# Token index stored behind each row, a new order of the first steps, and x of eight tiles transposed by VectorE through DRAM

## The reference

```
tid = clip(token_ids, 0, 24999);  expert = min(tid // 6250, 3)
h   = layernorm(x)
g   = silu(h @ ctx[e].T);  u = h @ ctx[e].T;  y = (g * u) @ ctx[e]      # e: the token's expert
x   = x + tanh(g_xattn) * y
h   = layernorm(x)                                                      # second half
out = x + tanh(g_ffn) * ((silu(h @ gate.T * gate_s) * (h @ up.T * up_s)) @ down.T * down_s)
```

## Time and profile before

| | |
|---|---|
| time, median of 3 runs (range) | 388.78 us (388.47 to 388.99) |
| profiled execution, its own time | 389.44 us |
| its span, first to last instruction | 387.7 us |
| TensorE busy | 373.1 us, 96% |
| VectorE busy | 243.5 us, 63% |
| ScalarE busy | 147.1 us, 38% |
| GpSimd busy | 81.8 us, 21% |
| DMA | 40.91 MB, mean 106 GB/s |

### The profile page before, as it was taken

The page is one execution under the profiler, slowest core; times in us unless marked ns, Lnnn a source line. Parts: engine busy times, 40 slices in busy tenths (PEclk is TensorE's granted clock), DMA queues, the critical chain, the costliest instruction groups (busy, mean ns, idle before and its releaser), DMA issues.

```text
span 387.7 us, 5617 instructions
## 1 busy us (share of the span) xinstructions
PE 373.1 (96%) x1757; PEld 303.1 (78%) x1757; DVE 243.5 (63%) x455; ACT 147.1 (38%) x265; POOL 81.8 (21%) x108
## 2 busy tenths in 40 slices
PE   3999999999999999999999999999999999999992
PEld 2477788888888878888888888888888888888891
DVE  6888856667877678778847255747246757222253
ACT  4355556565545346422332223332222332222220
POOL 7523443434352120010002101002101001200011
PEclk9999999999999999999999999999999999999997
DMA  6775666663221126333201322200232300100011
GB/s 221 258 253 191 248 216 253 210 216 102 89 68 68 56 86 216 97 119 81 83 0 54 135 80 83 71 11 31 88 124 62 101 27 27 81 0 0 0 41 73
DMA packets 21905, 40.91 MB, mean 106 GB/s; under 512 B 2672, under 2 KB 8816, under 8 KB 21888
## 3 DMA queue, kind: packets, MB, share of 16 engines
q1 hardware_dynamic: 17536, 26.50, 21.3%
q0 software_dynamic: 4352, 14.19, 9.8%
HBM read 28.36 MB, written 12.32 MB: 105 GB/s over the span
## 4 chain that ended last, share of the span: by engine, by line
PE 93%; DVE 3%; POOL 1%; issue 1%; ACT 0%; DVEq 0%; POOLq 0%
PE bank L1149 40%; PE bank L1045 26%; PE bank L1156 20%; PE bank L1031 2%; PE bank L1060 2%; PE bank L1073 1%; POOL minus_j L362 1%; PE bank L1021 0%; DVE rows L934 0%; PE bank L1012 0%; DVE tmp L927 0%; DVE xn L927 0%; DVE is_low L647 0%; PE bank L1083 0%; DVE sh L882 0%
## 5 line engine op out<-in xcount | busy, mean ns | idle before, releaser
L1149 PE MATMUL bank<-work,wgu 128*128 (+1 forms) x736 | 167.3, 380 | 0.0
L1149 PEld LDWEIGHTS bank<-work,wgu 128*128 128x128 f32 x736 | 133.9, 188 | 27.1 <-issue 0.5
L1045 PE MATMUL bank<-work,parts 128*128 (+1 forms) x432 | 110.7, 402 | 0.8 <-ACT parts L463 0.2
L1045 PEld LDWEIGHTS bank<-work,parts 128*128 128x128 f32 x432 | 78.5, 188 | 20.0 <-issue 2.9
L1156 PE MATMUL bank<-work,hp 128*128 128x512 f32 x352 | 87.2, 390 | 0.2 <-DVE hp L886 0.2
L1156 PEld LDWEIGHTS bank<-work,hp 128*128 128x128 f32 x352 | 65.7, 188 | 14.4 <-DVE hp L886 0.6
L867 DVE SCALAR_TENSOR_TENSOR sh<-bank,gs,sh 128x512 f32<-128x512 f32 x42 | 31.5, 749 | 55.6 <-PE bank L1149 55.6
L567 ACT ACTIVATE hp<-sh 128x512 fp32r<-128x512 f32 x42 | 26.6, 634 | 78.7 <-DVE sh L867 78.7
L562 ACT ACTIVATE sh<-bank,gs 128x512 f32<-128x512 f32 x42 | 28.9, 689 | 71.6 <-PE bank L1149 68.8
L391 POOL TENSOR_TENSOR rstd<-ve,half 128x1 f32<-128x1 f32 x31 | 18.1, 583 | 124.3 <-DVE ve L708 124.3
L446 POOL DMA_INDIRECT out<-rows,oidx x16 | 16.2, 1011 | 128.0 <-DVE rows L934 105.8
(11 more groups left out here) (132 smaller groups left out, 267.4 us busy)
## 6 DMA issues: line engine op xcount, KB each, us to landing
wraw<-guT SPq DMA_DIRECT2D x8, 704.0 KB
ctx_in<-ctxT SPq DMA_DIRECT2D x4, 1024.0 KB, 6.1
rows<-x_rows SPq DMA_DIRECT2D x8, 512.0 KB, 4.4
turned_rows<-xn SPq DMA_DIRECT2D x12, 256.0 KB, 2.7
rows<-turned_rows SPq DMA_DIRECT2D x12, 256.0 KB, 2.7
checked<-dwT SPq DMA_DIRECT2D x11, 256.0 KB
rows<-dwT SPq DMA_DIRECT2D x11, 256.0 KB, 2.9
rows<-x,gidx POOLq DMA_INDIRECT x19
```

Of the source, the lines that this page charges most:

```text
L1045: mm = pe.matmul(out_ps[:, :], part(s)[:, c * P:(c + 1) * P], ctx_w(e, c, w), start=n == 0, stop=n == last)
L1149: mm = pe.matmul(out_ps[:, tiles.start * P:tiles.stop * P], wgu[:, row + h, w, c * P:(c + 1) * P], moving, start=n == 0, stop=n == last)
```

## The change

- **Index behind each row.** Rows in SBUF and in the scratch tensor grow from 512 to 528 words (`WIDE`). GpSimd copies the token's index into word 512 of its slot (`token_in`); it travels with the row, and the last scatter reads it there. `oidx`, its VectorE operations, its 16 matmuls and the wait for it go away.
- **First steps.** Seven of the 16 low parts of the expert matrices move to GpSimd (`ON_POOL`); the nine left on VectorE are placed one by one, all but the last five ahead of x of tile 0's low part. x of tile 0 is normalised, transposed, rounded and subtracted in two halves, in two PSUM banks. `keep_busy` runs 11 and 2 matmuls instead of 15 and 3.
- **x of tiles 11 to 18** (`ON_PE` = 11) is no longer transposed by TensorE: norm(k+2) writes it in a permuted order, SP writes it to DRAM and reads it back (`turn_rows(0)` to `turn_rows(7)`), VectorE transposes 32x32 blocks (`turn`), ScalarE and VectorE split it (`turned_hi`, `turned_lo`). From step 10 on normalisation and statistics run one tile further ahead.
- **What is moved.** `first_stats(0)` and `(1)` both stand ahead of step 9, the other two behind steps 11 and 13. On SP the two halves of the load of block 0 are apart: one ahead of check row 8, the other behind `turn_rows(0)`; all eight `turn_rows` stand ahead of the down rows.

```diff
+WIDE = D + 16
+ON_PE = 11
+AHEAD = STEPS - ON_PE
+ON_POOL = [(1, 2), (1, 3), (2, 0), (2, 1), (2, 2), (3, 0), (3, 1)]
-    scratch = nc.dram_tensor("x1_rows", [2 * TOKENS + STEPS * P, D], F32).ap()
+    scratch = nc.dram_tensor("x1_rows", [2 * TOKENS + STEPS * P, WIDE], F32).ap()
-        rows = sb("rows", [P, ROWS, D], F32)
+        rows = sb("rows", [P, ROWS, WIDE], F32)
...
 (SP)
+            load_half(0, 0)
             check_row(8)
-            load_rows(0)
-            for c in range(9, IC):
-                check_row(c)
+            turn_rows(0)
+            load_half(0, 1)
+            check_row(9)
+            turn_rows(1)
+            check_row(10)
+            for n in range(2, AHEAD):
+                turn_rows(n)
...
 (GpSimd)
+            def ctx_lo(n_from, n_to):
+                for n in range(n_from, n_to):
+                    e, c = ON_POOL[n]
+                    pool.wait_ge(S["ctx_hi"], KC * e + c + 1)
+                    pool.tensor_tensor(ctx_w(e, c, 1), ctx_in[:, e, c, :], ctx_w(e, c, 0).bitcast(F32),
+                                       ALU.subtract).then_inc(S["pool_ctx_lo"], 1)
+            token_in(0, 2)
+            token_in(2, 4)
             inverse_std(1)
+            pool.wait_ge(S["xn_ready"], 2)
+            ctx_lo(0, 2)
+            inverse_std(2)
             gather(4)
-            inverse_std(2)
+            pool.wait_ge(S["xn_ready"], 3)
+            ctx_lo(2, 5)
+            inverse_std(3)
...
             store(0)
+            ctx_lo(5, 7)
             for k in range(2, STEPS + 1):
-                if k + 2 < STEPS:
+                if k < ON_PE:
                     inverse_std(k + 2)
...
                     gather(k + 4)
+                    token_in(k + 4)
+                if ON_PE - 1 <= k < STEPS - 3:
+                    inverse_std(k + 3)
...
 (VectorE)
+            def last_on_pe(k):
+                h_lo(k - 1)
+                norm(k + 1, ring_slot(k + 1))
+                landed(k + 2)
+                stats(k + 2, ring_slot(k + 2))
+                hidden(k)
+                x_lo(k + 1)
+                norm(k + 2, ring_slot(k + 2))
+                update(k - 1)
+                landed(k + 3)
+                stats(k + 3, ring_slot(k + 3))
+            def step(k):
+                h_lo(k - 1)
+                if k + 2 < STEPS:
+                    norm(k + 2, ring_slot(k + 2))
+                if k + 1 > ON_PE:
+                    turn(k + 1 - ON_PE, True)
+                hidden(k)
+                if k + 1 == ON_PE:
+                    turn(0, True)
+                if k + 3 < STEPS:
+                    landed(k + 3)
+                    begin_stats(ring_slot(k + 3))
+                turned_lo(k + 1)
+                if k + 3 < STEPS:
+                    end_stats(k + 3)
+                update(k - 1)
...
-            for k in range(EXPERTS, STATS_AT):
+            for k in range(EXPERTS, ON_PE - 2):
+                step_on_pe(k)
+            first_stats(0)
+            first_stats(1)
+            last_on_pe(ON_PE - 2)
+            for k in range(ON_PE - 1, NORM_AT):
                 step(k)
-            for k in range(STATS_AT, NORM_AT):
-                step(k)
-                first_stats(k - STATS_AT)
+                if k % 2:
+                    first_stats((k - STATS_AT) // 2 + 2)
...
 (TensorE)
-            keep_busy(15)
-            turn_x(0)
-            keep_busy(3)
-            first_product(0, 0, ctx_ready=KC)
-            pe.wait_ge(S["low_ready"], 3)
-            pe.wait_ge(S["route_sb"], 4)
-            for c in range(CT):
-                mm = pe.matmul(bank[4][:, 0:TILES], is_low[:, :, c], in_tile[:, 0, 0:TILES, c],
-                               start=c == 0, stop=c == CT - 1)
+            keep_busy(11)
+            for c in range(KC):
+                pe.wait_ge(S[("first_half", "xn_ready")[c // 2]], 1)
+                mm = pe.transpose((xt_ps, ht_ps)[c // 2][:, c * P:(c + 1) * P], xn[:, c * P:(c + 1) * P], ident[:, :])
+            keep_busy(2)
+            first_product(0, 0, ctx_of=0, half_ready=(S["xhi_half"], 1))
...
-            with pe.Fori(EXPERTS, 15) as k:
+            with pe.Fori(EXPERTS, ON_PE - 1) as k:
+                expert_step(k, *experts_at(k), turns=True)
+            with pe.Fori(ON_PE - 1, 15) as k:
                 expert_step(k, *experts_at(k))
```

More of the change, by code:

```diff
@@ L53 @@
 TURN_AT = {c + 2: t for c, t in PREP_AT.items()}
-TURNED = TILES - BLOCK
+ON_PE = 11
+AHEAD = STEPS - ON_PE
+TURNED = AHEAD + TILES - BLOCK
 QUADS = 4
+ON_POOL = [(1, 2), (1, 3), (2, 0), (2, 1), (2, 2), (3, 0), (3, 1)]
+ON_VECTOR = [(e, c) for e in range(EXPERTS) for c in range(KC) if (e, c) not in ON_POOL]
+HALF = D // 2
 def ring_slot(k):
@@ L201, in token_half, with token_of, first_xt @@
             return slice(i * D // 2, (i + 1) * D // 2)
+        def token_of(first, last):
+            return rows[:, first:last, D:D + 1].bitcast(U32)
+        def first_xt(i):
+            return (xt_ps, ht_ps)[i][:, i * HALF:(i + 1) * HALF]
         def gate_ps(i):
@@ L513, in _ @@
             ctx_hi(1)
-            x_hi(0)
+            for i, (done, ready) in enumerate((("xt_half", "xhi_half"), ("xt_done", "xhi_ready"))):
+                act.wait_ge(S[done], 1)
+                act.activation(tile_x(0)[:, i * HALF:(i + 1) * HALF], first_xt(i), ACT.Copy)\
+                   .then_inc(S[ready], 1)
             ctx_hi(2, range(0, 2))
@@ L524, in _, with step @@
             ctx_hi(3)
[L526 removed]
+            def step(k, on_pe=False):
                 h_hi(k - 1)
@@ L530, in step @@
                 silu(k)
-                x_hi(k + 1)
-            with act.Fori(PIECES_AT, IC + PIECES_AT) as k:
+                if on_pe:
+                    x_hi(k + 1)
+                else:
+                    turned_hi(k + 1)
+            with act.Fori(PIECES_AT, ON_PE - 1) as k:
+                step(k, on_pe=True)
+                down_check(k - PIECES_AT)
+            with act.Fori(ON_PE - 1, IC + PIECES_AT) as k:
                 step(k)
@@ new lines, in first_x_halves, with first_x_low_halves @@
+            def first_x_halves():
+                dve.wait_ge(S["rstd_ready"], 1)
+                for i, ready in enumerate(("first_half", "xn_ready")):
+                    part = slice(i * HALF, (i + 1) * HALF)
+                    dve.tensor_scalar(xn[:, part], rows[:, ring_slot(0), part], mv[:, 0, 0:1], rstd[:, 0:1],
+                                      ALU.subtract, ALU.mult).then_inc(S[ready], 1)
+            def first_x_low_halves():
+                for i, ready in enumerate(("xhi_half", "xhi_ready")):
+                    part = slice(i * HALF, (i + 1) * HALF)
+                    dve.wait_ge(S[ready], 1)
+                    low = dve.tensor_tensor(tile_x(1)[:, part], first_xt(i), tile_x(0)[:, part].bitcast(F32),
+                                            ALU.subtract)
+                low.then_inc(S["xlo_ready"], 1)
@@ L811, in _ @@
             x_lo(1)
-            for k in range(1, EXPERTS):
-                step_with_ctx(k)
-            dve.wait_ge(S["route_pe"], 5)
-            dve.tensor_copy(oidx[:, :], bank[4][:, 0:TILES]).then_inc(S["oidx_ready"], 1)
-            for k in range(EXPERTS, STATS_AT):
+            ctx_lo(5, 6)
+            norm(2, ring_slot(2))
+            h_lo(0)
+            hidden(1)
+            x_lo(2)
+            landed(3)
+            stats(3, ring_slot(3))
+            dve.wait_ge(S["gates_ready"], 1)
+            update(0)
+            ctx_lo(6, 7)
+            norm(3, ring_slot(3))
+            h_lo(1)
+            hidden(2)
+            x_lo(3)
+            landed(4)
+            stats(4, ring_slot(4))
+            update(1)
+            norm(4, ring_slot(4))
+            ctx_lo(7, 9)
+            h_lo(2)
+            hidden(3)
+            x_lo(4)
+            landed(5)
+            stats(5, ring_slot(5))
+            update(2)
+            for k in range(EXPERTS, ON_PE - 2):
[4 more added lines that the diff above has]
+            for k in range(ON_PE - 1, NORM_AT):
                 step(k)
-            for k in range(STATS_AT, NORM_AT):
-                step(k)
-                first_stats(k - STATS_AT)
+                if k % 2:
+                    first_stats((k - STATS_AT) // 2 + 2)
             step(14)
```

243 lines of the change are left out of this document (128 added, 115 removed).

## The result

| | before | after |
|---|---|---|
| time, median of 4 runs (range) | 388.66 us (388.47 to 388.99) | 385.20 us (384.71 to 385.73) |
| profiled execution, its own time | 389.44 us | 384.71 us |
| its span | 387.7 us | 382.6 us |

The ratio is 0.9904, 95% interval 0.9887 to 0.9921: the change makes the kernel 3.5 us faster, 1.0%. The forecast was 382.9 us, a gain of 5.9; the time lies inside the range. In three of the kernels further down (stats_later, ctx3_late, all_start) one execution is more than 1.5% above the fastest; their medians and ranges include it, the ratios don't.

The account below looks back on a forecast made before the run. TensorE, busy 96%, was taken as the bound. 3.5 (start) + 3.5 (turns) - 1.0 (step 9) - 0.1 (tile 11) = 5.9 us off 389.44 gave 383.5, and 382.9 us for the median; range 380.9 to 386.0.

Parts of the forecast that it names:

- Start of the first product: First expert product on TensorE starts at 15.3 us instead of 16.49, 1.2 us earlier; its 0.5 us stall goes.
- Step 0 to step 1: Step 1 starts at 20.9 us instead of 22.43, after ScalarE's high parts of expert 2; 1.5 us gained so far.
- Steps 1 to 3: GpSimd's low parts, 1.25 us each, remove TensorE's waits; 0.4 us stall remains in step 1; 1.95 us gained.
- Eight turns: Tiles 11 to 18 lose their transposes on TensorE, 0.44 us a set, 3.5 us in all.
- Step 9: A second first_stats on VectorE delays tile 10's normalisation; TensorE stands 1.0 us.
- Tile 11: In step 10, its x returns through DRAM after 5 us; 0.1 us lost, 1.6 us if 6.9.
- Tile 12: Its write queues behind the block load's second half and a check row; rows 1.5 us later, still about +3.0 of step 11.
- (a): Rival: the stalls of steps 9 and 1 are covered; 1.4 us more gain, 381.5 us; chance 0.16.
- (b): Rival: first steps don't yield, GpSimd's low parts cost 2.5 us or engines block each other; 385.9 us; chance 0.12.
- (c): Rival: first product on TensorE slow without four busy-keeping matmuls; 2.8 us lost, 385.7 us; chance 0.04.
- (d): Rival: VectorE is the bound in steps 11 to 17, 0.3 us each; 385.0 us; chance 0.12.
- (e): Rival: DRAM round trip becomes the period over eight steps; at 8.7 us, 392.4 us, slower; chance 0.04.

Follow-up runs that it names:

- stats_later: Changed kernel with first_stats(1) behind step 10 instead of ahead of step 9; 385.52 us.
- ctx3_late: Like both_norm, with expert 3's matrix loaded only once tile 2's rows have landed; 383.80 us, ratio to before 0.9873.
- all_start: Like both_norm, plus the earlier word reads, tile 1's earlier low part and the later load of expert 3's matrix; 383.39 us, ratio to before 0.9857.
- words: Like both_norm, with TensorE reading the two packed words of expert numbers ahead of x of tile 1's turn; 383.42 us, ratio to before 0.9861.
- words_xlo: Like words, with tile 1's low part on VectorE ahead of tile 2's gather wait and statistics; 382.58 us, ratio to before 0.9833.
- kb3: Changed kernel with 3 busy-keeping matmuls instead of 11 ahead of x of tile 0; 386.79 us, ratio to before 0.9951.
- load_first: Changed kernel with the second half of the block load ahead of turn_rows(0) on SP; 384.28 us, ratio to before 0.9880.
- both_norm: Kernel with both moves, and in step 9 tile 11's normalisation ahead of tile 10's low part; 384.31 us.
- the start alone: Changed kernel with x of tiles 11 to 18 transposed by TensorE, first_stats and block load placed as before the change; 386.70 us, ratio to before 0.9924.
- both moves: Changed kernel with the edits of load_first and stats_later together; 383.92 us, ratio to before 0.9865.

## Why the prediction was right, and where it was off

The sign and the range held, the size was 5.9 us against 3.5 measured by the medians and 4.15 up to the MLP in the profile. The 0.7 us between these two are differences between executions that the traces don't place. By its steps:

- **Start of the first product:** 15.3 forecast, 15.31 measured; its stall gone. The power took 0.58 us instead of 0.96 and the high part 0.35 us a half, as taken; the statistics started 0.07 us later than before and not 0.25 (11.98 against 11.91).
- **Step 0 to step 1:** the start at 20.9 was right (20.99), the reason was not. ScalarE's high parts, which should have held silu until 19.07, began at 17.36 instead of 17.88 and silu at 18.42. TensorE waited for its own two reads, as the words kernel shows. That agreement is luck: ScalarE was 0.6 us earlier than forecast, and the reads, which the prediction doesn't have, took it up. Counting the index matmuls at nothing looked only at VectorE's product behind them and not at these reads.
- **Steps 1 to 3:** 3.5 us by step 4 forecast, 3.55 measured. The stall of step 1 had the right size (0.4 forecast, 6.82 against 6.41 us measured) and the right order of VectorE's list, but the statistics of tile 2 were late because their gather took 6.3 us to land, a path that the prediction doesn't name. That is why the earlier turn of h in the words kernel gained nothing by step 1. GpSimd's part took 1.25 us, as taken from the iota's 1.2 ns per element. The estimate from the Trainium skill (GPSIMD Engine Reference, section 3.1), 1.1 us, is a little low. The exclusion between VectorE and GpSimd, of which the Trainium skill speaks (SBUF — State Buffer, Who interferes with whom), showed in the power and in no low part: 0.93 and 1.04 us where a low part of VectorE had started before it (words_xlo, all_start), 0.54 to 0.59 for one column in nearly all other places. Twice it took 0.78 and 0.90 us (kb3 at 113.09, all_start at 110.86) beside a VectorE normalisation, which reads one tile and not two.
- **Eight turns:** 0.44 us each was too small. The intervals fall from 6.43 to 5.91 to 5.93, 0.5 us a turn, 4.2 in all: the transposes cost their 0.44, and 24 matmuls in a row take 5.47 us in the chain, 0.07 less than twice 2.77 with a turn between.
- **Step 9:** 1.0 forecast, 0.93 measured, by the mechanism named, and taken away by moving one first_stats.
- **Tile 11, the term that failed:** forecast 0.1 us, measured 1.90 by the first product and up to 2.14 by the interval, which has part of tile 12's delay in it. The normalisation ended where I put it (79.02, +6.43 of the step). The round trip was 6.5 us and not 5: I took the landing times of the MLP, where no gathers run, though the prediction had its own upper end of 6.9 us with 1.6 us of stall beside it. To this come 0.45 us from the end of ScalarE's part (87.32) to TensorE's start (87.77), 0.44 or 0.45 also in load_first, both_norm and words; for tiles 13 to 18 the same handover takes 0.03 to 0.20 us in these traces. What fills it at tile 11 isn't settled.
- **Tile 12:** I had named the 528 KB and the check row ahead of its write, and put 1.5 us on it, with the rows back at +3.0 of step 11 and no stall; the write took 4.9 us, 2.2 more than the median of 2.7, the rows came at +4.1 of step 11, and TensorE lost 0.83 us (0.56 of it in the interval of step 12). Moving the load took that away.
- **Tiles 13 to 18:** no stall forecast, none measured. VectorE did not become the bound.
- **The MLP** was taken as untouched, and up to the last matmul it is (240.9 against 241.0 us). In the trace of the start alone it is 1.5 us longer, by a wait that hangs on the last stores and the down rows. The prediction didn't look there.

Of the rivals, none took place as a whole: (a) did not, both stalls were there; (b) fell with GpSimd's 1.25 us, (c) was 0 with eleven matmuls and 0.3 us in the trace with three, (d) did not occur. (e) named the right resource, the DRAM round trip, but it decides only for the first two tiles, where the lead is short, not as a period.

## What to carry to other kernels

A step that leaves the bound engine for a path through DRAM is paid at its first tiles: check the first one's lead against the round trip under the traffic that runs there, not against the same transfer elsewhere in the kernel, and judge a new order by the whole round trip, since a faster write came with a slower read here. Two things placed ahead of the entry (a statistics step on VectorE, and a block load that stood between two writes on the queue) cost 0.93 and 0.83 us, and moving them was free. Before shortening the start, ask which landing it waits for: here a turn of h that came 0.6 us earlier was worth nothing, because the next step waited for a gather. When a filler is removed from a bound engine, ask what the filler hid on that engine's own sequencer.

## What the runs showed of the hardware

- A 256 KB write through SP's queue lands in 2.3 us, in 3.8 us when an indirect gather of 256 KB was issued 0.8 us earlier on GpSimd's queue, and in 4.9 us behind a 528 KB load and a 256 KB one on its own queue (3.7 us without the 528 KB). Where the write was fast, 3.5 to 4.5 us passed from the issue of the read to VectorE's transposes, instead of 2.6 to 2.7.
- An indirect gather of 256 KB landed in 3.3 us at the shortest and 7.5 us at the longest; that of tile 2, issued at 14.0 us, took 5.7 to 7.1 us.
- With two reads of a word into TensorE's registers directly ahead of a turn, the turn starts 0.74 to 0.90 us after its input is there; with the reads one turn earlier, or with the input 0.9 us or more later, 0.05 us after it.
- After 3.1 us of idleness TensorE took 1.06 us for two matmuls that took 0.59 us after a busy stretch, with a granted clock of 1.00 in the profile's rows in both.
- After a wait of 1.5 us in the kernel with both moves, the granted clock was 0.57 for 2.6 us and 0.75 for 2.3 us, and matmuls started 0.43 us apart instead of 0.23; after a wait of 1.6 us at the same place in ctx3_late it stayed at 1.00.
